# Scan stage of a fused tokenizer, state-space and expert kernel: part of the multiply by C moved from VectorE to GpSimd

## The chip, the cores and the metric

One core of one Trainium2 chip runs the whole program. The metric is the device time of one execution in microseconds (us). Of this kernel a difference of about 0.3%, or 4 us, can be told from none.

## What is computed

The reference is a model in three parts: a tokenizer over 32 images, a state-space block with a gated feed-forward, and attention with a mixture of experts. The change lies in the state-space block, in its selective scan:

```python
xdbl = jnp.einsum('bld,kd->blk', z, W_xproj)
dt_in, Bm, Cm = jnp.split(xdbl, [DT_RANK, DT_RANK + D_STATE], axis=-1)
dt = jax.nn.softplus(jnp.einsum('blr,dr->bld', dt_in, W_dt) + b_dt)
A_bar = jnp.exp(dt[..., None] * A)
Bx = (dt * z)[..., None] * Bm[:, :, None, :]
_, h = jax.lax.associative_scan(comb, (A_bar, Bx), axis=1)   # h = A_bar * h + Bx
y = jnp.einsum('blds,bls->bld', h, Cm) + D_skip * z
```

There are 16 states, an inner width of 384 and 82 tokens per sequence. Everything is float32.

## The kernel before

The 32 sequences go in 8 rounds of G = 4. A round's tokens are N = 4 x 82 = 328 columns. The inner width lies on 128 partitions in NI = 3 tiles, so that one state of a round is a row of 3 x 328 = 984 columns, cut into two halves of HALF = 492.

For each state `s` of a round the engines do this, each in a queue written out by hand:

- ScalarE (`decays`, L1208) writes exp(dt A) into PSUM, half by half, two states ahead.
- GpSimd (`inputs`, L1452) writes Bx = dtz x B into a ring of four tiles in SBUF, three states ahead.
- VectorE (`scan`, L1340) scans each half into the PSUM tile `hs`. Then (`step`, L1352) it multiplies `hs` by the row of C: first the columns 0 to 656 (semaphore `s_hm`), then 656 to 984 (`s_hc`), into one of the four tiles of `hc`. Then it scans state s+1, whose first half waits for `s_hm` and its second half for `s_hc`.
- TensorE (`add_y`, L1069) adds the two halves of `hc` into the PSUM sum of y with an identity matrix. It waits for `s_hc` once and counts `s_ys`. The ring of four keeps VectorE from writing `hc` of state s before `s_ys` has passed state s-4.

Between these steps each engine has the work of the next round (`pre`) and of the round before (`post`), placed by state number. Of it these pieces matter here. TensorE and ScalarE do theirs ahead of the step of the same state, VectorE and GpSimd behind it:

- After state 15 ScalarE copies y out of PSUM (`drain`, L1226). Only then may TensorE add state 0 of the next round (L1069). At state 1 it multiplies y by W_out (L1025), and VectorE adds the result to the input in two parts (L1316).
- At state 2 TensorE transposes (L977). At states 3, 4 and 5 it makes the gate and the input of the next round (L983, L986). ScalarE takes the tanh (L1155), and VectorE makes z of it (L1295), which frees the PSUM bank for the next one. At state 6 come the projections X (L1007), and ScalarE keeps them (L1159, L1160). At state 8 TensorE makes the step sizes D0 and D1, at state 9 D2 (L990). ScalarE takes rl and ax of each (L1133, L1134) and behind D2 also `u` (L1167).
- At states 3 and 4 ScalarE squares x1 and makes the mean (`b_ms`, L1185), and GpSimd's `post` of state 4 waits for it (`b_rr`, L1437). GpSimd's `post` of state 6 are two adds (L1441).
- GpSimd's step of state 10 waits for `u` of the next round. Behind it come the product for state 13 and then the softplus of the next round on GpSimd (L1422 to L1432), between the products for 14 and 15.
- At states 10 to 13 TensorE makes the feed-forward's gate and up parts (L983, L986), ScalarE the tanh (L1198) and VectorE the two products th and av (L1321, L1324). At state 14 TensorE makes the down projection (L1050).

Round 0 stands ahead of the loop, rounds 1 to 6 are three turns of a loop with two rounds in each, and round 7 stands behind it. SyncE loads the rows of B and C for the next round into `BC`, group by group of four states, when `s_hc` says that the old ones are read.

Of the kernel before, what the change touches and what calls it, by code (L numbers as in the profile page):

```python
# [776 lines left out]
def mamba(nc, ctx, block, at, ps, tok, fr, H, vec, ident, w_zg, w_x, w_dt, a_log, w_o, w_ug, w_dn, bc_d, xs):  # L777
# [4 lines left out]
    if True:  # L782
# [485 lines left out]
        def _(v):  # L1268
# [78 lines left out]
            def step(i, par, s, last):  # L1347
                v.wait_ge(s_scan, 2 * (i * STATE + s) + 2)
                at_least(v, s_ys, i * STATE + (s - LONG + 1))
                C = CL[:, s % GROUP, :] if par == 1 and s // GROUP == 3 else BC[:, s // GROUP, 1, s % GROUP, :]  # L1350
                for a, b, done in ((0, 2, s_hm), (2, 3, s_hc)):
                    v.tensor_tensor(hc[:, s % LONG, a:b], hs.rearrange("p (a n) -> p a n", a=NI)[:, a:b],  # L1352
                                    C.rearrange("p (a n) -> p a n", a=1).broadcast_to([128, b - a, N]), ALU.mult).then_inc(done, 1)
# [1303 lines left out]
```

## Time and profile before

| | |
|---|---|
| median of 3 runs | 1356.89 us (1353.74 to 1357.17) |
| profiled execution, its own time | 1359.36 us |
| its span | 1357.3 us |
| scan stage in it | from about 246 to 758 us |
| granted TensorE clock, mean | 0.941 |
| busy over the span | PE 88%, DVE 79%, ACT 52%, POOL 54% |

PE is TensorE, DVE is VectorE, ACT is ScalarE, POOL is GpSimd. A timeline row gives the start in us from the span's beginning, the length in us of the merged instructions, the engine, the line, the operation, its operands and the count. In brackets stands how long the engine was idle before it, and what ended that.

### The profile page before, as it was taken

Reading aid. Unit: us, or ns where it says so; the run is one execution under the profiler, and the core shown is the slowest. Engines: PE = TensorE matmul, PEld = TensorE weight load, DVE = VectorE, ACT = ScalarE, POOL = GpSimd, SP = SyncE. Lnnn points to the kernel's source line nnn. Section 1 sums busy time; section 2 is a strip of 40 time slices with the busy share of each in tenths; the row PEclk is TensorE's granted clock in tenths of the full one; section 3 lists DMA queues with packets and bytes.
Section 4 is the critical chain, followed back from the end, with each engine's and each line's share of the span. In section 5 each row is a group of like instructions: output and inputs, shape, how many; then the busy total and the mean of one; then the engine's idle time right before and its main releaser. Section 6 shows DMA issues by size and latency. Waiting matters only on the chain.

```text
span 1357.3 us, 20617 instructions
## 1 busy us (share of the span) xinstructions
PE 1192.2 (88%) x5716; PEld 754.8 (56%) x5717; DVE 1067.9 (79%) x2393; ACT 702.1 (52%) x1628; POOL 739.3 (54%) x465
## 2 busy tenths in 40 slices
PE   6985867568998889898987789999999889999996
PEld 4432434224444445455443468888888666676674
DVE  5999697989999899989999646778887646666663
ACT  1256431776776778676856345555552462233232
POOL 3047662877888686959696410135555565222322
PEclk9997878798999999999999899999997789999998
DMA  6200002651615152423430044001112133222221
GB/s 176 71 1 0 28 9 61 240 190 40 221 33 206 28 202 81 149 87 143 140 123 0 1 143 138 9 17 25 26 26 55 34 59 53 41 39 38 38 39 22
DMA packets 76919, 102.83 MB, mean 76 GB/s; under 512 B 13562, under 2 KB 65369, under 8 KB 76825
## 3 DMA queue, kind: packets, MB, share of 16 engines
q1 hardware_dynamic: 57490, 90.82, 20.4%
q0 software_dynamic: 17152, 9.24, 5.1%
q10 hardware_dynamic: 2184, 1.72, 0.5%
q8 instruction: 35, 0.57, 0.2%
q14 instruction: 58, 0.48, 0.1%
HBM read 70.23 MB, written 30.18 MB: 74 GB/s over the span
## 4 chain that ended last, share of the span: by engine, by line
PE 56%; DVE 19%; ACT 12%; issue 9%; POOL 2%; DMA 1%; DVEq 1%; SPq 0%; ACTq 0%; POOLq 0%
PE ps L1069 6%; PE ps L2298 6%; PE ps L2276 5%; DVE ps L1340 3%; PE ps L1713 3%; ACT ps L1208 3%; PE ps L1050 3%; PE ps L1655 3%; PE ps L2281 3%; PE ps L983 3%; PE ps L1728 3%; PE ps L2288 3%; PE ps L277 2%; PE ps L270 2%; DVE hc L1352 2%
## 5 line engine op out<-in xcount | busy, mean ns | idle before, releaser
L1452 POOL TENSOR_TENSOR Bx<-dtz,BC 128x984 f32<-128x984 f32 x128 | 289.6, 2288 | 77.1 <-DVE ps L1340 46.1
L1069 PE MATMUL ps<-hc,b_id 128*128 128x492 f32 x512 | 249.0, 612 | 61.6 <-DVE hc L1352 47.0
L1340 DVE TENSOR_TENSOR_SCAN ps<-ps,Bx 128x492 f32<-128x492 f32 x256 | 288.4, 1172 | 6.9 <-POOL Bx L1452 5.8
L1208 ACT ACTIVATE ps<-dt,A 128x324 f32<-128x324 f32 (+1 forms) x512 | 213.1, 457 | 51.5 <-DVE ps L1340 50.6
L1069 PEld LDWEIGHTS ps<-hc,b_id 128*128 128x128 f32 x512 | 91.8, 195 | 174.1 <-issue 120.6
L2434 POOL DMA_INDIRECT out<-yt,dest x48 | 74.8, 1558 | 160.6 <-DVE yt L2420 150.7
L2353 ACT ACTIVATE hT__6165<-ps,e_b 128x128 f32<-128x128 f32 x288 | 79.4, 374 | 154.1 <-PE ps L2288 154.0
L1352 DVE TENSOR_TENSOR hc<-ps,BC 128x656 f32<-128x656 f32 x224 | 139.1, 663 | 5.3 <-PE ps L1069 1.5
L2298 PE MATMUL ps<-W,hT__6165 128*128 x576 | 109.5, 327 | 1.1 <-DVE yb L2414 1.1
L2129 POOL DMA_INDIRECT buckets<-XS,c_slot x64 | 90.6, 1416 | 32.0 <-issue 15.8
L2298 PEld LDWEIGHTS ps<-W,hT__6165 128*128 128x128 f32 x576 | 91.7, 191 | 1.7 <-issue 1.7
L2141 POOL TENSOR_TENSOR c_x<-c_x,bro 82x192 f32<-82x192 f32 x32 | 18.9, 590 | 135.3 <-DVE c_x L1896 134.6
L2400 DVE COPY hb<-ps 128x768 f32<-128x768 f32 x41 | 39.2, 957 | 58.7 <-PE ps L2281 56.4
L2276 PE MATMUL ps<-W,xT 128*128 x192 | 78.8, 535 | 6.8 <-DVE xT L2391 2.7
L1869 DVE TENSOR_REDUCE mx<-ps 82x12 f32<-82x984 f32 x32 | 37.7, 1178 | 52.5 <-PE ps L1713 51.7
L1728 PEld LDWEIGHTS ps<-V,PT 82*82 82x82 f32 x768 | 62.5, 156 | 7.4 <-issue 1.8
L1713 PE MATMUL ps<-kB,qT 128*82 128x328 f32 (+1 forms) x256 | 61.9, 387 | 3.1 <-DVE E L1873 2.0
L1728 PE MATMUL ps<-V,PT 82*82 82x17 f32 x768 | 61.4, 226 | 0.7 <-DVE XN L1903 0.7
L579 POOL TENSOR_TENSOR DF<-DF,prod 96x392 f32<-96x392 f32 x56 | 56.6, 1010 | 4.4
L983 PE MATMUL ps<-hfT,wug 128*128 128x328 f32 x128 | 45.4, 479 | 14.5 <-DVE av L1324 13.0
L207 DVE SCALAR_TENSOR_TENSOR ps<-PF,vec,ps 96x196 f32<-96x196 f32 (+2 forms) x168 | 57.7, 424 | 0.0
L207 DVE SCALAR_TENSOR_TENSOR ps<-P,vec,ps 128x196 f32<-128x196 f32 x168 | 56.4, 421 | 0.0
(283 smaller groups left out, 2415.9 us busy)
## 6 DMA issues: line engine op xcount, KB each, us to landing
BC<-bc_rows SPq DMA_DIRECT2D x16, 1312.0 KB, 9.2
BC<-bc_rows SPq DMA_DIRECT2D x28, 656.0 KB, 6.9
buckets<-b_zero SPq DMA_DIRECT2D x8, 2288.0 KB, 14.8
xg<-buckets SPq DMA_DIRECT2D x48, 104.0 KB
xc<-in_xcol SPq DMA_DIRECT2D x4, 1176.0 KB, 9.4
W<-in_w1d SPq DMA_DIRECT2D x8, 576.0 KB, 10.2
W<-in_w2d SPq DMA_DIRECT2D x8, 576.0 KB, 10.3
CL<-bc_rows SPq DMA_DIRECT2D x4, 656.0 KB, 8.2
```

The costliest lines, as they stand in the source:

```text
L207: i = eng.scalar_tensor_tensor(flat(dst[:, k, cols]) if t == 8 else acc, tap(src, k, c, t, a, b), w, acc, ALU.mult, ALU.add)
L983: pe.matmul(ps[:, banks[k], 0:N], w[:, k, c_], x[:, 0, :], start=True, stop=False)
L1069: mm = pe.matmul(ps[:, BANK_Y + h, 0:HALF], ident[:], f2(hc[:, s % LONG])[:, h * HALF:(h + 1) * HALF], start=s == 0, stop=s == STATE - 1)
L1208: a = act.activation(ps[:, BANK_A + h, c:c + w].rearrange("p (g t) -> p g t", t=S)[:, :, 1:S], dt[:, (par + t // STATE) % 2, m, g0 * S:g1 ...
L1340: v.tensor_tensor_scan(hs[:, c], ps[:, BANK_A + h, 0:HALF], f2(Bx[:, t % RING])[:, c], 0.0, ALU.mult, ALU.add).then_inc(s_scan, 1)
L1352: v.tensor_tensor(hc[:, s % LONG, a:b], hs.rearrange("p (a n) -> p a n", a=NI)[:, a:b], C.rearrange("p (a n) -> p a n", a=1).broadcast_to( ...
L1452: g.tensor_tensor(Bx[:, t % RING], dtz[:, p], BC[:, t % STATE // GROUP, 0, t % GROUP, :].rearrange("p (a n) -> p a n", a=1).broadcast_to([ ...
L1713: mm = pe.matmul(ps[0:S, SCORES + h0 // 6, (h0 % 6) * S:(h0 % 6 + h1 - h0) * S], qT[:, par, m_, q * S:(q + 1) * S], kB[:, par, m_, q, j:j ...
L1728: mm = pe.matmul(ps[0:S, HEAD_OUT + c % 2, h * (DH + 1):(h + 1) * (DH + 1)], PT[:, c % 2, h, :], V[:, vpar, c, h, :], start=True, stop=True)
L2129: g.indirect_dma_start(out=xs, out_offset=bass.IndirectOffsetOnAxis(ap=slot[:, p % 2, k, c:c + 1], axis=0), in_=slots(p)[:, c, :], in_offs ...
L2276: pe.matmul(ps[:, UP + h, 0:384], xT[:, p, 0, :], W1[:, bass.ds(e, 1), h * 384:(h + 1) * 384].rearrange("p a n -> p (a n)"), start=True, s ...
L2298: mm = pe.matmul(ps[:, Y, 0:D], hT[:, p, k, :], W2[:, k, bass.ds(e, 1), :].rearrange("p a n -> p (a n)"), start=k == 0, stop=k == KF - 1)
```

## The change

In the seven states of `POOLED` the second half is scanned straight into the tile of `hc` in SBUF. VectorE multiplies only the first half, in two instructions of 328 and 164 columns. GpSimd multiplies the second half in place, in two instructions of 164 and 328 columns. It does so at its step of the next state, ahead of the product Bx that stood there, and counts `s_hp`. TensorE waits for `s_hp` between the two halves of such a state. The first half scan behind a state of `POOLED` waits for `s_hc` instead of `s_hm`, and the second half scan of a state of `POOLED` has to wait for its tile of `hc` (`s_ys`) itself. SyncE waits for `s_hp` too before it loads new rows of C.

```diff
+        POOLED = (0, 1, 2, 3, 5, 7, 8)
...
+        def pooled(i, s):
+            return i * len(POOLED) + sum(k < s for k in POOLED)
...
                 for h in range(2):
+                    if h == 1 and s in POOLED:
+                        pe.wait_ge(s_hp, pooled(i, s) + 1)
                     mm = pe.matmul(ps[:, BANK_Y + h, 0:HALF], ident[:], f2(hc[:, s % LONG])[:, h * HALF:(h + 1) * HALF],
...
-                    at_least(v, s_hc if h else s_hm, i * STATE + t)
+                    at_least(v, s_hc if h or (t - 1) % STATE in POOLED else s_hm, i * STATE + t)
+                    direct = h == 1 and t % STATE in POOLED
+                    if direct:
+                        at_least(v, s_ys, i * STATE + (t - LONG + 1))
                     c = slice(h * HALF, (h + 1) * HALF)
-                    v.tensor_tensor_scan(hs[:, c], ps[:, BANK_A + h, 0:HALF], f2(Bx[:, t % RING])[:, c],
+                    v.tensor_tensor_scan((f2(hc[:, t % LONG]) if direct else hs)[:, c], ps[:, BANK_A + h, 0:HALF], f2(Bx[:, t % RING])[:, c],
                                          0.0, ALU.mult, ALU.add).then_inc(s_scan, 1)
...
+                if s in POOLED:
+                    v.tensor_tensor(out[:, 0:N], hs[:, 0:N], C, ALU.mult).then_inc(s_hm, 1)
+                    v.tensor_tensor(out[:, N:HALF], hs[:, N:HALF], C[:, 0:HALF - N], ALU.mult).then_inc(s_hc, 1)
...
             def step(i, par, s, last):
+                if s - 1 in POOLED:
+                    C, out = rows_c(par, s - 1), f2(hc[:, (s - 1) % LONG])
+                    g.wait_ge(s_scan, 2 * (i * STATE + s))
+                    g.tensor_tensor(out[:, HALF:2 * N], out[:, HALF:2 * N], C[:, HALF - N:N], ALU.mult)
+                    g.tensor_tensor(out[:, 2 * N:3 * N], out[:, 2 * N:3 * N], C, ALU.mult).then_inc(s_hp, 1)
```

The two places of which the prediction speaks most are GpSimd's queue from the start of a round to its wait for b_ms and beyond, and TensorE's queue at states 7 to 9. First GpSimd, in a turn of the loop, before: the products for states 4, 5 and 6, then b_rr.

```order
79 L1452 TENSOR_TENSOR Bx<-dtz,BC 128x984 [waits b_scan]
80 L1447 ISA
81 L640 ISA [waits b_BC1]
82 L1452 TENSOR_TENSOR Bx<-dtz,BC 128x984 [waits b_scan]
83 L640 ISA
84 L1452 TENSOR_TENSOR Bx<-dtz,BC 128x984 [waits b_scan]
85 L640 ISA
86 L1452 TENSOR_TENSOR Bx<-dtz,BC 128x984 [waits b_scan]
87 L640 ISA
88 L1452 TENSOR_TENSOR Bx<-dtz,BC 128x984 [waits b_scan]
89 L1437 TENSOR_TENSOR b_rr<-b_ms,b_nh 82x4 [waits b_mss]
```

And now, from behind the pair for state 0 on: before each product stands a pair of multiplies by C.

```order
101 L1471 TENSOR_TENSOR Bx<-dtz,BC 128x984 [waits b_scan,b_BC1]
102 L1485 ISA
103 L1486 TENSOR_TENSOR hc<-hc,BC 128x164 [waits b_scan]
104 L1487 TENSOR_TENSOR hc<-hc,BC 128x328
105 L1471 TENSOR_TENSOR Bx<-dtz,BC 128x984 [waits b_scan]
106 L1485 ISA
107 L1486 TENSOR_TENSOR hc<-hc,BC 128x164 [waits b_scan]
108 L1487 TENSOR_TENSOR hc<-hc,BC 128x328
109 L1471 TENSOR_TENSOR Bx<-dtz,BC 128x984 [waits b_scan]
```

Four pairs now stand ahead of b_rr, for the states 0 to 3. The pairs for 5, 7 and 8 stand between b_rr and the wait for u.

TensorE at states 7 to 9, before: add_y of state 7, D0 and D1, add_y of state 8, D2.

```order
195 L1065 REGISTER_ALU
196 L1069 MATMUL ps<-hc,b_id 128x492 x2
197 L990 MATMUL ps<-dtin,wdt 128x328 x2
198 L1065 REGISTER_ALU
199 L1069 MATMUL ps<-hc,b_id 128x492 x2
200 L990 MATMUL ps<-dtin,wdt 128x328
```

And now:

```order
219 L1075 REGISTER_ALU
220 L1081 MATMUL ps<-hc,b_id 128x492
221 L1080 REGISTER_ALU
222 L1081 MATMUL ps<-hc,b_id 128x492
223 L1000 MATMUL ps<-dtin,wdt 128x328 x2
224 L1075 REGISTER_ALU
225 L1081 MATMUL ps<-hc,b_id 128x492
226 L1080 REGISTER_ALU
227 L1081 MATMUL ps<-hc,b_id 128x492
228 L1000 MATMUL ps<-dtin,wdt 128x328
```

The two halves of a state are now parted by a register operation and the wait for GpSimd, and D0, D1 and D2 stand behind such waits.

## Rows read from the trace of the kernel before

**Rows 1.** The page's chain that ended last, shares by engine.

```profile
PE 56%; DVE 19%; ACT 12%; issue 9%; POOL 2%; DMA 1%; DVEq 1%; SPq 0%; ACTq 0%; POOLq 0%
```

**Rows 2.** Windows, u to u: length, busy PE, PEld, DVE, ACT, POOL, clock, DMA.

```profile
479.75:542.39 62.64, 58.23 (x213) 31.41 (x212) 60.54 (x80) 47.46 (x112) 51.56 (x24) 1.00 0.36 124
542.39:609.66 67.27, 59.74 (x213) 32.03 (x212) 60.84 (x80) 47.20 (x112) 51.54 (x25) 0.97 0.34 116
```

**Rows 3.** Groups by shape, VectorE in the scan stage; count, then busy us, mean ns.

```profile
L1352 DVE TENSOR_TENSOR hc<-ps,BC 128x656 f32<-128x656 f32 x112 | 93.6, 836 | 5.3 <-PE ps L1069 1.5 <-issue 1.2
L1352 DVE TENSOR_TENSOR hc<-ps,BC 128x328 f32<-128x328 f32 x112 | 54.8, 489 | 0.0
```

**Rows 4.** Timeline of GpSimd, from the start of round 4 to u.

```profile
497.03 18.04 POOL L1452 TENSOR_TENSOR Bx<-dtz,BC 128x984 f32<-128x984 f32 x8
517.99 2.28 POOL L1452 TENSOR_TENSOR Bx<-dtz,BC 128x984 f32<-128x984 f32 x1 [2.92 <-DVE ps L1340]
523.29 1.02 POOL L1437 TENSOR_TENSOR b_rr<-b_ms,b_nh 82x4 f32<-82x4 f32 x1 [3.02 <-ACT b_ms L1185]
528.80 1.97 POOL L1441 TENSOR_TENSOR x<-x,H 82x384 f32<-82x384 f32 x2
530.72 4.50 POOL L1452 TENSOR_TENSOR Bx<-dtz,BC 128x984 f32<-128x984 f32 x2
542.39 2.32 POOL L1452 TENSOR_TENSOR Bx<-dtz,BC 128x984 f32<-128x984 f32 x1 [4.10 <-ACT u L1167]
```

**Rows 5.** Line 1441's view: GpSimd's queue, duration ns min/median/max.

```profile
L1441 POOLq FUSED_REGOPS  x12: 60/60/60, 334.7 to 657.4; - x12
```

**Rows 6.** Timeline of VectorE, the same round.

```profile
505.77 1.23 DVE L1352 TENSOR_TENSOR hc<-ps,BC 128x656 f32<-128x656 f32 x2
506.92 2.25 DVE L1340 TENSOR_TENSOR_SCAN ps<-ps,Bx 128x492 f32<-128x492 f32 x2
514.03 0.55 DVE L1316 TENSOR_TENSOR x<-xl,ps 82x384 f32<-82x384 f32 x1 [0.88 <-PE ps L1025]
533.69 2.25 DVE L1340 TENSOR_TENSOR_SCAN ps<-ps,Bx 128x492 f32<-128x492 f32 x2
535.98 1.25 DVE L1352 TENSOR_TENSOR hc<-ps,BC 128x656 f32<-128x656 f32 x2
```

**Rows 7.** Timeline of TensorE, the same round.

```profile
508.21 1.89 PE L1069 MATMUL ps<-hc,b_id 128*128 128x492 f32 x4 [1.17 <-ACT y L1226]
509.93 4.06 PE L1025 MATMUL ps<-wo,y 128*82 128x192 f32 x24
521.81 1.37 PE L983 MATMUL ps<-hT,wzg 128*128 128x328 f32 x4
539.03 0.72 PE L990 MATMUL ps<-dtin,wdt 96*128 96x328 f32 x2
```

**Rows 8.** Timeline of ScalarE, the same round.

```profile
521.40 0.85 ACT L1208 ACTIVATE ps<-dt,A 128x162 f32<-128x162 f32 x2 [0.21 <-DVE ps L1340]
531.33 0.44 ACT L1159 ACTIVATE BCs<-ps 32x328 f32<-32x328 f32 x1 [1.66 <-PE ps L1007]
540.22 0.53 ACT L1133 ACTIVATE rl<-ps,vec 128x328 f32<-128x328 f32 x1
541.20 1.02 ACT L1167 ACTIVATE u<-ax 128x984 f32<-128x984 f32 x1
```

**Rows 9.** Timelines of GpSimd and TensorE at rounds 0, 5 and 7.

```profile
245.83 17.90 POOL L1452 TENSOR_TENSOR Bx<-dtz,BC 128x984 f32<-128x984 f32 x8 [2.29 <-DVE dtz L1309]
...
285.18 2.32 POOL L1452 TENSOR_TENSOR Bx<-dtz,BC 128x984 f32<-128x984 f32 x1 [3.93 <-ACT u L1167]
...
590.56 1.02 POOL L1437 TENSOR_TENSOR b_rr<-b_ms,b_nh 82x4 f32<-82x4 f32 x1 [3.03 <-ACT b_ms L1185]
...
609.66 2.28 POOL L1452 TENSOR_TENSOR Bx<-dtz,BC 128x984 f32<-128x984 f32 x1 [4.10 <-ACT u L1167]
...
734.24 1.27 PE L983 MATMUL ps<-hfT,wug 128*128 128x328 f32 x4
```

More of the change, by code:

```diff
@@ L822, in mamba @@
         s_w1 = sem("b_w1"); s_c1 = sem("b_c1"); s_sp = sem("b_sp"); s_dt = sem("b_dt"); s_dtz = sem("b_dtz")
-        s_ab = sem("b_ab"); s_bx = sem("b_bx"); s_scan = sem("b_scan"); s_hc = sem("b_hc"); s_hm = sem("b_hm"); s_ys = sem("b_ys"); s_skip = sem("b_skip"); s_y = sem("b_y")
+        s_ab = sem("b_ab"); s_bx = sem("b_bx"); s_scan = sem("b_scan"); s_hc = sem("b_hc"); s_hm = sem("b_hm"); s_hp = sem("b_hp"); s_ys = sem("b_ys"); s_skip = sem("b_skip"); s_y = sem("b_y")
         s_o = sem("b_o"); s_x1 = sem("b_x1"); s_sq = sem("b_sqs"); s_ms = sem("b_mss"); s_rr = sem("b_rr2"); s_hf = sem("b_hf"); s_tr2 = sem("b_tr2")
@@ L832, in f2, with rows_c @@
             return t.rearrange("p a b -> p (a b)")
+        def pooled(i, s):
+            return i * len(POOLED) + sum(k < s for k in POOLED)
+        def rows_c(par, s):
+            return CL[:, s % GROUP, :] if par == 1 and s // GROUP == 3 else BC[:, s // GROUP, 1, s % GROUP, :]
         SIDE_TILES = [("O0", 0, s_x1, 2, 1), ("O1", 0, s_x1, 2, 2), ("RT0", 1, s_hT, 2, 1), ("RT1", 1, s_hT, 2, 2),
@@ L922, in _ @@
                     sp.wait_ge(s_hc, old + 4)
+                    sp.wait_ge(s_hp, pooled(j - 1, 4))
                 spread(0)
@@ L929, in _ @@
                     sp.wait_ge(s_hc, old + 8)
+                    sp.wait_ge(s_hp, pooled(j - 1, 8))
                 spread(1)
@@ L938, in _ @@
                     sp.wait_ge(s_hc, old + 12)
+                    sp.wait_ge(s_hp, pooled(j - 1, 12))
                 spread(2, slice(1, 2))
@@ L1349, in step @@
                 at_least(v, s_ys, i * STATE + (s - LONG + 1))
[L1350 to L1353, printed above, removed]
+                C, out = rows_c(par, s), f2(hc[:, s % LONG])
+                if s in POOLED:
+                    v.tensor_tensor(out[:, 0:N], hs[:, 0:N], C, ALU.mult).then_inc(s_hm, 1)
+                    v.tensor_tensor(out[:, N:HALF], hs[:, N:HALF], C[:, 0:HALF - N], ALU.mult).then_inc(s_hc, 1)
+                else:
+                    for a, b, done in ((0, 2, s_hm), (2, 3, s_hc)):
+                        v.tensor_tensor(hc[:, s % LONG, a:b], hs.rearrange("p (a n) -> p a n", a=NI)[:, a:b],
+                                        C.rearrange("p (a n) -> p a n", a=1).broadcast_to([128, b - a, N]), ALU.mult).then_inc(done, 1)
                 if not last or s + 1 < STATE:
```

## Prediction

> **What bounds the scan stage now.** I read the chain that ended last first. It is a chain of TensorE more than of VectorE [rows 1], although the windows show VectorE busy for 60.5 of 62.6 us of a round and TensorE for 58.2 [rows 2]. So I looked for what ties one round to the next, in the timelines of one round, number 4. The tie is `u`: GpSimd stands idle for 4.10 us until ScalarE has it [rows 4], then makes the softplus and, 17.3 us later, the product for state 15, for which VectorE's scan of state 15 waits. From there two paths lead to the next `u`. One is VectorE's scans and multiplies. The other is TensorE's: y out of PSUM at 508.21, state 0, the W_out product at 509.93, the gates, X, and then ScalarE from 531.33 to u at 541.20 [rows 7, 8]. That stretch of ScalarE shows no idle time in front of its rows behind the first, so only an earlier X or an earlier D2 could move u, and X hangs on TensorE's queue. VectorE waits 0.88 us for the W_out product at 514.03 [rows 6]. A lighter VectorE alone would therefore wait more there and gain little. GpSimd has waits of 2.92, 3.02 and 4.10 us in the round [rows 4], which is the room that the change wants to use. A round takes 62.6 us, or 67.3 where the loop turns [rows 2].
>
> **What VectorE saves.** The multiply of 656 columns takes 836 ns and that of 328 takes 489 ns, so a column costs 1.06 ns [rows 3]. 492 columns less are 0.52 us per state. The first scan now waits for the second multiply: without a wait it starts 0.08 us before the listed end (505.77 + 1.23 against 506.92), with one an instruction starts 0.04 us behind it (533.69 + 2.25 against 535.98) [rows 6]. That takes 0.12 us back. Net 0.4 us per state, 2.8 per round, 22 over the eight rounds, all of it beside the path above except in round 7. A scan into SBUF instead of PSUM is in no row for this shape; I price it at no difference, with bounds of 0.1 us either way, for which VectorE's room is the cover.
>
> By the Trainium skill, page "VectorE: DVE Perf Modes", section "The DRAIN you can't avoid", a semaphore wait on the engine's own last operation costs nothing extra. The rows here show 0.12 us; by the page VectorE would save 29 us instead of 22, and the forecast would stay, since that time is not on the path.
>
> **What GpSimd gets.** Products of 984 columns follow each other at 18.04 / 8 = 2.255 us, adds of 384 at 1.97 / 2 = 0.985 us [rows 4]. A straight line through both gives 0.17 us plus 2.12 ns per column: 0.52 and 0.87 us, a pair 1.39. The listed sums contain the tail of the last instruction, so I take 1.35. Bounds: 1.13 us, which is half a product of 984 columns with no fixed cost at all, and 1.97 us, two instructions at the price of the 384-column adds. Seven pairs are 9.5 us in each round on an engine that was busy for 51.6 of 62.6: 61.0 of 62.6.
>
> The page "GPSIMD Engine Reference" of the Trainium skill, sections 3.1 and 4.1, says that two-input elementwise work takes GpSimd 2.6 cycles per element and should stay on VectorE. At the 4497 ns it gives for 2048 columns, an estimate for a pair without fixed cost is 1.08 us. The rows give 1.35; by the page the sum below would be some 3 us smaller.
>
> **Where the pairs stand on the path, round 4.**
> 1. State 0. GpSimd makes five products from 497.03 to 508.3, then the pair, to 509.65. TensorE wants the second half in the middle of 508.21 to 509.93, at 509.05 [rows 7]. It starts 0.65 us late, with a handover of 0.05. The W_out product and VectorE's x1 at 514.03 follow, +0.65. Up to X, 0.25 of it is won back: the gate at 521.81 waited for z on VectorE, which now comes earlier. So X and BCs at 531.33 are 0.4 late, and u could not be less than 0.4 late.
> 2. b_rr. Products and four pairs take GpSimd from 497.03 to 522.7, so it still waits for b_ms. That stands behind the decays at 521.40, which waited for the scan [rows 8]. ScalarE starts its piece 0.65 late but no longer waits, so b_rr comes at about 523.7 instead of 523.29.
> 3. States 5, 7, 8. From b_rr to the end of the two products at 530.72 + 4.50 it was 11.9 us. With three pairs it is 16.0, so the pair of state 8 ends at 539.7. The pairs of states 1, 2, 3 and 5 are done before TensorE wants them; state 7's is about 2 us late but D0 and D1 still arrive when ScalarE gets to them.
> 4. D2. TensorE takes the second half at 539.75, 0.85 us, and D2 starts at 540.6 instead of 539.03 [rows 7] and ends at 541.15. ScalarE's rl, at 540.22 before [rows 8], starts at 541.15. **u, and with it the round, is 0.9 us later.** VectorE's 2.8 us become waits: for the decays, for th and av, and for Bx of state 15.
>
> **The other rounds.** Where the loop turns (1, 3, 5), y is copied later than GpSimd is done with state 0, so step 1 costs nothing, and b_rr comes 0.2 earlier, at 590.35, by the 0.21 that the decays waited for the scan [rows 8, 9]. Then 16.0 + 0.9 + 0.6 put the end of D2 at 607.85; rl stood at 609.66 - 2.17 = 607.49, by the distance of rows 4 and 8. That is +0.35 each. Round 0 has no b_rr: 245.83 + 12 x 2.255 + 7 x 1.35 = 282.3, D2 ends at 283.75, and u reaches GpSimd 2.1 us later, at 285.9 instead of 285.18 [rows 9], +0.7. In round 7 the first feed-forward gate at 734.24 stands behind the same queue and comes 1.7 us later; VectorE had 1.2 us of room before it needed that gate, so +0.45.
>
> **Sum.** 0.7 + 3 x 0.35 + 3 x 0.9 + 0.45 = 4.9 us. To it come TensorE's new register operations between the halves: a register operation on a queue takes 60 ns [rows 5], five per round lie on TensorE's path, so between 0 and 8 x 0.3 = 2.4 us; I take 1. Together **+6 us**. SyncE's new waits cost nothing: the rows of C that they guard are for the next round, more than 20 us off. The profiled execution took 1359.4 (span 1357.3) and would take 1365; the median of the runs is 2.5 us below that execution, so I predict **1363 us**, 0.4% slower. A measurement of this kernel can tell about 0.3% from no change, 4 us; "same" below means within that. A pair of 1.13 us instead of 1.35 takes some 0.65 off at D2: only the floor of 0.4 in rounds 2, 4, 6 and nearly nothing else are left, 1358. A pair of 1.97 makes GpSimd arrive at b_rr behind b_ms: 2 x 0.6 for the pairs and 1.8 behind it, about +3.5 per round, 1385.
>
> **Rivals.**
> - *Faster: the pair of state 8 is no obstacle.* If a pair took under about 0.85 us, state 0's would end by 509.1 and state 8's before 538.2, where TensorE wants it (D2's 539.03 less 0.85), and no wait would be left on the path. Then the earlier z and the earlier scan win some 0.3 us in each of seven rounds, and round 7, where little but VectorE counts, gains its 2.8. That is 5 us, 1352. For it: GpSimd's idle time of 10 us a round is as long as the seven pairs. Against it: 1.13 us is the least that the rows allow. If I am wrong about TensorE and ScalarE holding u, part of VectorE's 22 us would show too, down to 1335. Chance 0.18.
> - *No change: the waits cancel.* Pairs near 1.13 us, or b_ms earlier than I think, so that the delays fall below 0.4 us a round. 1358. Chance 0.30.
> - *Much slower: the pairs are dear.* GpSimd and VectorE hold each other up in SBUF, or each short instruction costs 0.3 us more. From a pair of 1.5 us on GpSimd is late at b_rr too and bounds every round. At 2 us a pair it is 1388. Against it: the products ran at 2.25 us each while VectorE was busy 97% of the time. Chance 0.10. [...]
> - *The change doesn't do what it says.* The queues show the pairs and the waits, so I give this nothing.
>
> **How the numbers follow.** The forecast itself, slower by 4 to 20 us, has 0.42. Faster by over 0.3%: 0.18. Within: 0.30. Slower: 0.42 + 0.10 = 0.52. The range of the forecast alone is 1361 to 1377. For 8 in 10 I go from 1350, below the first rival's 1352 but not to its 1335, to 1379, short of the dear pairs.
>
> **What would show it.** Right: GpSimd's idle before u falls from 4.1 us to about 1; waits of TensorE's L1081 and its weight loads for GpSimd's hc at states 7 and 8; D2 about 1.5 us later after b_rr; VectorE with some 3 us of new idle time a round; rounds of 63.5 and 67.6 us; pairs of 0.5 and 0.85 us. Wrong: a round shorter than 62.6 us; no wait for hc of GpSimd on TensorE; GpSimd's wait before b_rr gone, which would mean that the pairs are dearer.

## The result, and the profile after

The changed kernel takes **1367.22 us** (median of 5 runs, 1364.68 to 1369.88) against 1356.89 (5 runs, 1352.55 to 1360.88). The ratio is 1.0083, 95% interval 1.0061 to 1.0106: 0.8% slower, +10.3 us, where +6 was forecast. The profiled execution took 1369.88 us, span 1368.0; it is the slowest of the five runs. (One execution of the experiment e1 took 1449 us at a mean granted clock of 0.809, against 0.93 to 0.95 in all others, and is left out of its ratio.)

The chain that ended last, after. GpSimd's share has gone from 2% to 20% [rows 1].

```profile
PE 46%; POOL 20%; DVE 14%; issue 11%; ACT 6%; DMA 1%; DVEq 0%; POOLq 0%; SPq 0%; ACTq 0%
```

Windows after, u to u, with the columns of [rows 2]: a round is 1.1 us longer, or 0.4 where the loop turns. VectorE has lost 2.65 us of work (60.54 to 57.89) and GpSimd has gained 9.1.

```profile
481.52:545.25 63.73, 57.97 (x213) 31.36 (x212) 57.89 (x80) 47.12 (x112) 60.67 (x39) 1.00 0.37 122
545.25:612.89 67.64, 59.11 (x213) 32.05 (x212) 57.90 (x80) 47.02 (x112) 60.64 (x38) 0.97 0.34 116
```

Groups by shape after, in the scan stage. The two GpSimd multiplies have 0.54 and 0.88 us; in the timeline they start 0.50 apart and the next instruction 0.84 later, so a pair occupies 1.34 (1.35 was taken). The scan into SBUF is not slower than the one into PSUM: the 56 are all second halves and most of the 199 first ones, but the distance from the start of a state's first scan to its multiply is 2.28 us with it and 2.29 without.

```profile
L1355 DVE TENSOR_TENSOR_SCAN ps<-ps,Bx 128x492 f32<-128x492 f32 x199 | 227.8, 1178 | 20.8 <-ACT ps L1220 12.6 <-POOL Bx L1471 3.3 <-DVE hc L1368 0.9
L1355 DVE TENSOR_TENSOR_SCAN hc<-ps,Bx 128x492 f32<-128x492 f32 x56 | 64.6, 1154 | 0.0
L1487 POOL TENSOR_TENSOR hc<-hc,BC 128x328 f32<-128x328 f32 x56 | 49.4, 881 | 0.0
L1486 POOL TENSOR_TENSOR hc<-hc,BC 128x164 f32<-128x164 f32 x56 | 29.9, 535 | 10.2 <-DVE hc L1355 10.2
```

Waits after, rounds 1 to 6: engine, line, what it waited for, us in total, times, longest. These two rows have no counterpart before.

```profile
PEld ps L1081 <- POOL hc L1487: 26.5, 21, 2.4
PE ps L1081 <- POOL hc L1487: 13.2, 15, 1.6
```

VectorE after, the multiplies of one state and the scan behind them. From the first multiply to the scan it is 0.83 us, before it was 1.15 [rows 6].

```profile
507.59 0.49 DVE L1367 TENSOR_TENSOR hc<-ps,BC 128x328 f32<-128x328 f32 x1
508.00 0.32 DVE L1368 TENSOR_TENSOR hc<-ps,BC 128x164 f32<-128x164 f32 x1
508.42 1.19 DVE L1355 TENSOR_TENSOR_SCAN ps<-ps,Bx 128x492 f32<-128x492 f32 x1
```

Timeline of GpSimd after, round 4, which answers to [rows 4]: the pair of state 0, b_rr, the pair of state 8, Bx behind u, and the softplus's first row.

```profile
509.96 0.55 POOL L1486 TENSOR_TENSOR hc<-hc,BC 128x164 f32<-128x164 f32 x1
510.46 0.90 POOL L1487 TENSOR_TENSOR hc<-hc,BC 128x328 f32<-128x328 f32 x1
...
525.41 1.03 POOL L1456 TENSOR_TENSOR b_rr<-b_ms,b_nh 82x4 f32<-82x4 f32 x1 [1.09 <-ACT b_ms L1197]
...
539.97 0.52 POOL L1486 TENSOR_TENSOR hc<-hc,BC 128x164 f32<-128x164 f32 x1
540.47 0.87 POOL L1487 TENSOR_TENSOR hc<-hc,BC 128x328 f32<-128x328 f32 x1
...
545.25 2.30 POOL L1471 TENSOR_TENSOR Bx<-dtz,BC 128x984 f32<-128x984 f32 x1 [1.69 <-ACT u L1179]
547.51 3.52 POOL L1441 TENSOR_SCALAR ax<-u 128x984 f32<-128x984 f32 x1
```

Timeline of TensorE after, the same round, which answers to [rows 7]: state 0, the W_out product, states 7 and 8, D2. The waits of 0.19, 1.59 and 0.53 us are for GpSimd's multiplies. The pair of state 8 ends at 541.34, TensorE goes on at 541.38, and D2 stands right behind it.

```profile
510.16 1.06 PE L1081 MATMUL ps<-hc,b_id 128*128 128x492 f32 x2 [1.17 <-ACT y L1238]
511.41 1.09 PE L1081 MATMUL ps<-hc,b_id 128*128 128x492 f32 x2 [0.19 <-POOL hc L1487]
512.34 4.06 PE L1035 MATMUL ps<-wo,y 128*82 128x192 f32 x24
...
537.83 1.09 PE L1081 MATMUL ps<-hc,b_id 128*128 128x492 f32 x2 [1.59 <-POOL hc L1487]
...
541.38 1.09 PE L1081 MATMUL ps<-hc,b_id 128*128 128x492 f32 x2 [0.53 <-POOL hc L1487]
542.31 0.72 PE L1000 MATMUL ps<-dtin,wdt 96*128 96x328 f32 x2
```

**Where the 10 us come from.** I take the distance between the softplus's first rows on GpSimd (`ax<-u`, the last row of the fence above) as the length of a round, count round 0 from its first Bx, and end round 7 at the memset of kB. In us:

| round | 0 | 1 | 2 | 3 | 4 | 5 | 6 | 7 | stage |
|---|---|---|---|---|---|---|---|---|---|
| before | 41.8 | 64.3 | 62.7 | 67.4 | 62.7 | 67.2 | 62.7 | 81.8 | 510.5 |
| after | 43.8 | 65.3 | 63.7 | 69.1 | 63.7 | 67.6 | 63.7 | 84.4 | 521.3 |
| difference | 2.0 | 1.0 | 1.05 | 1.7 | 1.05 | 0.4 | 1.0 | 2.6 | 10.8 |
| forecast | 0.7 | 0.35 | 0.9 | 0.35 | 0.9 | 0.35 | 0.9 | 0.45 | 4.9 + 1 |

All of the loss is in the scan stage: what stands before and behind it took 846.7 us in both profiled executions (245.8 + 600.9 and 241.9 + 604.8). That rest is the same program in every kernel here, yet it varied from 838.8 (e1) to 850.9 us (e6) between profiled executions. So the stage is compared by its own length, and the kernels by the ratios of many runs.

Rounds 2, 4, 5 and 6 went nearly as forecast. The excess is in rounds 0, 1, 3 and 7. In 1, 3 and 7 rows of TensorE stand at a lower clock than before; in round 0 it is a wait. The end of round 7, TensorE after:

```profile
729.01 1.09 PE L1081 MATMUL ps<-hc,b_id 128*128 128x492 f32 x2 [0.44 <-DVE hc L1368]
732.42 2.74 PE L1081 MATMUL ps<-hc,b_id 128*128 128x492 f32 x4 [2.31 <-POOL hc L1487]
735.97 2.01 PE L1081 MATMUL ps<-hc,b_id 128*128 128x492 f32 x2 [0.81 <-POOL hc L1487]
737.77 3.03 PE L1074 MATMUL ps<-z,skip 128*128 128x328 f32 x8
...
742.28 1.27 PE L993 MATMUL ps<-hfT,wug 128*128 128x328 f32 x4
```

The skip product took 1.82 us before and takes 3.03 here; two additions of 492 columns take 2.01 instead of 1.09. The granted clock of this stretch, after (first window) and before (second, in a fence of its own), is 0.81 against 1.00, which is a mixture of the levels 2.4 and 1.2 GHz:

```profile
727.00:745.00 18.00, 14.43 (x41) 7.21 (x40) 14.20 (x19) 8.92 (x21) 17.88 (x13) 0.81 0.00 0
```

```profile
722.00:741.00 19.00, 15.45 (x52) 7.45 (x52) 18.83 (x24) 10.48 (x24) 15.34 (x10) 1.00 0.00 1
```

The feed-forward gate, at 742.28, is 63.45 us behind its round's softplus row; before it was 734.24 - 674.58 = 59.66 [rows 9]. VectorE then waits for th:

```profile
744.81 0.50 DVE L1333 SCALAR_TENSOR_TENSOR th<-th,ps 128x328 f32<-128x328 f32 x1 [3.40 <-ACT th L1210]
```

In round 0 TensorE reaches the pair of state 0 before GpSimd has it. The rows of TensorE after:

```profile
252.21 4.64 PE L1081 MATMUL ps<-hc,b_id 128*128 128x492 f32 x6 [2.79 <-POOL hc L1487]
256.69 0.73 PE L987 MATMUL ps<-b_id,hn 82*128 82x82 f32 x8
```

The transposition is now 256.69 - 241.90 = 14.8 us behind the round's first Bx, where it was 257.43 - 245.83 = 11.6. ScalarE's copy of it stands ahead of decays that VectorE needs, so VectorE waits 2.96 us at 259.72.

### The profile page after: what moved, and what is told of

Same layout as the page of the kernel before. It is cut to its first block, busy times and chain, and to the rows that moved or that the text cites. A ratio compares the mean times of both kernels' runs of the same rounds, so it can differ in the third digit from the quotient of the medians.

```text
span 1368.0 us, 20809 instructions
## 1 busy us (share of the span) xinstructions
PE 1198.4 (88%) x5716; PEld 759.3 (56%) x5717; DVE 1045.3 (76%) x2393; ACT 699.9 (51%) x1628; POOL 812.0 (59%) x577
## 3 DMA queue, kind: packets, MB, share of 16 engines
q10 hardware_dynamic: 2184, 1.72, 0.5%
## 4 chain that ended last, share of the span: by engine, by line
PE 46%; POOL 20%; DVE 14%; issue 11%; ACT 6%; DMA 1%; DVEq 0%; POOLq 0%; SPq 0%; ACTq 0%
POOL Bx L1471 11%; PE ps L2322 6%; PE ps L2300 5%; PE ps L1679 3%; PE ps L1737 3%; PE ps L2305 3%; PE ps L1752 3%; PE ps L2312 3%; PE ps L277 2%; PE ps L1081 2%; POOL hc L1487 2%; PE ps L270 2%; DVE ps L207 2%; ACT prod L398 2%; POOL hc L1486 2%
## 5 line engine op out<-in xcount | busy, mean ns | idle before, releaser
L1081 PE MATMUL ps<-hc,b_id 128*128 128x492 f32 x512 | 256.4, 620 | 70.3 <-POOL hc L1487 22.4
L1355 DVE TENSOR_TENSOR_SCAN ps<-ps,Bx 128x492 f32<-128x492 f32 x200 | 229.0, 1178 | 23.3 <-ACT ps L1220 12.6
L1220 ACT ACTIVATE ps<-dt,A 128x324 f32<-128x324 f32 (+1 forms) x512 | 210.5, 456 | 43.5 <-DVE ps L1355 40.1
L1371 DVE TENSOR_TENSOR hc<-ps,BC 128x656 f32<-128x656 f32 x112 | 69.5, 661 | 0.8
L1355 DVE TENSOR_TENSOR_SCAN hc<-ps,Bx 128x492 f32<-128x492 f32 x56 | 64.6, 1154 | 0.0
L1752 PE MATMUL ps<-V,PT 82*82 82x17 f32 x768 | 62.3, 227 | 0.7 <-DVE XN L1927 0.7
```

Source lines behind the costliest of these rows:

```text
L1220: a = act.activation(ps[:, BANK_A + h, c:c + w].rearrange("p (g t) -> p g t", t=S)[:, :, 1:S], dt[:, (par + t // STATE) % 2, m, g0 * S:g1 ...
L1355: v.tensor_tensor_scan((f2(hc[:, t % LONG]) if direct else hs)[:, c], ps[:, BANK_A + h, 0:HALF], f2(Bx[:, t % RING])[:, c], 0.0, ALU.mult, ...
L1752: mm = pe.matmul(ps[0:S, HEAD_OUT + c % 2, h * (DH + 1):(h + 1) * (DH + 1)], PT[:, c % 2, h, :], V[:, vpar, c, h, :], start=True, stop=True)
```

## The experiments

Times are medians; ratios are to the kernel before, run beside it on the same chip. Its own median was 1354.88 for e1 to e4, 1355.53 for e5 to e8, 1355.34 for e9 to e11 and 1357.67 for e12. To place a cost I divide round 4 into three pieces, at the W_out product and at b_rr; they are the first three columns. All numbers are distances between rows of GpSimd's and TensorE's timelines, in us:

| kernel | softplus to W_out | W_out to b_rr | b_rr to next softplus | stage | ratio |
|---|---|---|---|---|---|
| before | 27.93 | 13.36 | 21.38 | 510.5 | 1 |
| after | 28.54 | 13.07 | 22.10 | 521.3 | 1.0083 |
| e1 light VectorE | 27.18 | 13.05 | 21.22 | 501.8 | 0.9936 |
| e2 no TensorE wait | 27.37 | 13.16 | 21.12 | 502.6 | 0.9943 |
| e3 half later | 26.91 | 13.55 | 21.41 | 507.8 | 0.9991 |
| e4 without 7, 8 | 28.54 | 13.07 | 21.23 | 519.4 | 1.0045 |
| e5 only 5, 7, 8 | 28.08 | 13.36 | 22.04 | 514.9 | 1.0075 |
| e6 half later, 2 3 5 7 8 | 27.61 | 13.06 | 21.91 | 511.3 | 1.0006 |
| e7 pair of 8 twice | 29.15 | 13.07 | 23.47 | 535.7 | 1.0215 |
| e8 half later, 2 3 4 5 7 8 | 29.27 | 13.07 | 21.70 | 516.9 | 1.0084 |
| e9 half later, 0 1 2 3 5 | 26.77 | 13.67 | 21.33 | 505.9 | 0.9942 |
| e10 without 0 | 28.09 | 13.07 | 22.05 | 515.0 | 1.0044 |
| e11 half later, without 7 | 26.70 | 13.76 | 21.26 | 508.4 | 0.9992 |
| e12 half later, 0 to 3 | 26.65 | 13.85 | 21.26 | 506.4 | 0.9952 |

### e1: VectorE's saving alone

```diff
-                    if h == 1 and s in POOLED:
-                        pe.wait_ge(s_hp, pooled(i, s) + 1)
...
-                if s - 1 in POOLED:
...
-                    g.tensor_tensor(out[:, HALF:2 * N], out[:, HALF:2 * N], C[:, HALF - N:N], ALU.mult)
-                    g.tensor_tensor(out[:, 2 * N:3 * N], out[:, 2 * N:3 * N], C, ALU.mult).then_inc(s_hp, 1)
```

> The second half of the seven states is not multiplied by C at all: GpSimd's pairs, TensorE's waits for them and SyncE's are left out, VectorE's work stays as in the changed kernel. Theory (TensorE and ScalarE set the round, VectorE does not): little is won although VectorE has 22 us less work. Rounds from u to u of 62.3 to 62.6 us instead of 62.6, round 7 shorter by 2 to 3 us, together 4 to 7 us faster than before, about 1351. Rival A (VectorE sets the round): some 20 us faster, 1337. Rival B (the cost lies in VectorE's own new order, the scan that waits for the second multiply and the scans into SBUF): as slow as the changed kernel, 1367.

Measured: 1344.73 us, ratio 0.9936 (0.9914 to 0.9958), 9 to 10 us faster than before, more than the 4 to 7 expected. The stage is 8.7 us shorter, and each of rounds 2, 4 and 6 takes 61.45 instead of 62.68, where 62.3 to 62.6 were expected. So the saving is worth more than the 5 us that the first rival gave it, and far less than VectorE saves, which is 0.33 us a state or 18 us.

### e2: all the work, but TensorE doesn't wait for it

```diff
-                    if h == 1 and s in POOLED:
-                        pe.wait_ge(s_hp, pooled(i, s) + 1)
-                    mm = pe.matmul(ps[:, BANK_Y + h, 0:HALF], ident[:], f2(hc[:, s % LONG])[:, h * HALF:(h + 1) * HALF],
+                    mm = pe.matmul(ps[:, BANK_Y + h, 0:HALF], ident[:], f2(hc[:, s % LONG])[:, 0:HALF],
...
+                        at_least(v, s_hp, pooled(i + t // STATE, max(0, t % STATE - 3)))
```

> GpSimd makes all pairs in place as in the changed kernel, but TensorE adds the first half twice in place of the second, so it reads nothing of GpSimd's and has no wait for it; VectorE waits for the pair of four states ago instead, which is long done. Theory (the waits in TensorE's queue cost the time, not GpSimd's load): about as fast as the kernel with no pairs, 1351 to 1355, GpSimd's wait for u down to some 0.3 us. Rival (GpSimd's load of 61 us a round sets it, or holds VectorE up in SBUF): as slow as the changed kernel, 1364 to 1367, and scans or multiplies of VectorE longer than with no pairs.

Measured: 1346.73 us, ratio 0.9943 (0.9923 to 0.9962), within 2 us of e1 and faster than the 1351 to 1355 expected. GpSimd makes all its pairs and is nearly full; its wait for u falls to 0.69 us:

```profile
535.12 2.33 POOL L1471 TENSOR_TENSOR Bx<-dtz,BC 128x984 f32<-128x984 f32 x1 [0.69 <-ACT u L1177]
```

GpSimd's load by itself costs next to nothing. The 1.4% between this kernel and the changed one, some 19 us, are what the waits in TensorE's queue bring with them.

### e3: the second half added one step later

```diff
+                if s - 1 in POOLED:
+                    pe.wait_ge(s_hp, pooled(i, s - 1) + 1)
+                    half(s - 1, 1)
...
-                for h in range(2):
-                    if h == 1 and s in POOLED:
-                        pe.wait_ge(s_hp, pooled(i, s) + 1)
...
-                mm.then_inc(s_ys, 1)
+                half(s, 0)
+                if s not in POOLED:
+                    half(s, 1)
```

> The whole computation. TensorE takes the second half of a pooled state one step later, ahead of the first half of the next state, so D2 and the transposition stand ahead of the wait for the pair instead of behind it. Theory: D2 is no longer held up, u comes as before or 0.1 to 0.3 us earlier, rounds of 62.4 to 62.7 and 67.0 to 67.3 us, and round 7 gains 1 to 2 us: 1352 to 1356, that is 11 to 15 us below the changed kernel. Rival (any wait for GpSimd in TensorE's queue costs the same, wherever it stands, because GpSimd is behind): 1364 to 1367.

Measured: 1352.33 us, ratio 0.9991 (0.9973 to 1.0009). The whole computation stays, with the same seven pairs, and the loss is gone. The third column (b_rr to softplus) is back at 21.41. The only wait for a pair in round 4 behind the W_out product now stands behind D2 (at 533.73), where it can't hold u:

```profile
534.91 1.09 PE L1070 MATMUL ps<-hc,b_id 128*128 128x492 f32 x2 [0.37 <-POOL hc L1493]
```

### e4: without the pairs of states 7 and 8

```diff
-        POOLED = (0, 1, 2, 3, 5, 7, 8)
+        POOLED = (0, 1, 2, 3, 5)
```

> POOLED = (0, 1, 2, 3, 5), the whole computation. Theory (the pairs of 7 and 8 hold up D2, state 0's costs 0.4 us in rounds 2, 4 and 6 and about 2 us in round 0 through the transposition at state 2): rounds of 63.0 and 67.3 us, round 7 shorter than before by about 1, together +1 to +4 us, 1358 to 1361. Rival (cost in proportion to GpSimd's load): 5 of 7 pairs, +7 us, 1364.

Measured: 1359.80 us, ratio 1.0045 (1.0029 to 1.0062). The first two columns of the table are those of the changed kernel to a hundredth, and the third falls from 22.10 to 21.23: steps 3 and 4 of the prediction stand for 0.87 us a round. The trace also has the clock at work. Rounds 2 and 4 have the same wait for the pair of state 0 and the same addition ahead of the W_out product. In round 2 the clock falls, in round 4 not:

```profile
378.75 1.77 PE L1081 MATMUL ps<-hc,b_id 128*128 128x492 f32 x2 [0.64 <-POOL hc L1487]
380.31 5.11 PE L1035 MATMUL ps<-wo,y 128*82 128x192 f32 x24
```

```profile
511.37 1.09 PE L1081 MATMUL ps<-hc,b_id 128*128 128x492 f32 x2 [0.64 <-POOL hc L1487]
512.29 4.06 PE L1035 MATMUL ps<-wo,y 128*82 128x192 f32 x24
```

That is 1.05 us on the product and 0.68 on the addition, and round 2 lasts 64.5 us where round 4 lasts 62.8. Round 6 is like round 2: 4.93 us for the product, 64.6 for the round.

### e5: only the pairs of 5, 7 and 8

```diff
-        POOLED = (0, 1, 2, 3, 5, 7, 8)
+        POOLED = (5, 7, 8)
```

> POOLED = (5, 7, 8), the whole computation; the complement of the run without 7 and 8. Theory (the pairs of 7 and 8 stand ahead of D2): round 0 about 0.5 us shorter than before, since GpSimd is not behind there, rounds 2, 4 and 6 at 63.2, rounds 1, 3 and 5 0.3 us longer, round 7 1 to 2.5 us longer with TensorE's clock down behind its waits: +3 to +5 us, 1358 to 1360. Rival (only the load of GpSimd counts, 3 of 7 pairs, or only state 0's wait does): no slower than before.

Measured: 1364.73 us, ratio 1.0075 (1.0050 to 1.0100). That is above the 1358 to 1360 expected, though rounds 2, 4 and 6 have 63.5 us (63.2 expected) and round 7 is only 0.7 longer than before (1 to 2.5 expected). It is the counterpart of e4: the first half of the round is near the kernel before (41.44 against 41.29), the third column has the full 22.04. Its stage is 6.4 us shorter than the changed kernel's, but the ratio is nearly as bad. The profiled executions stand at opposite ends here: e5's is the fastest of its four runs, the changed kernel's the slowest of its five.

### e6: second half later, without states 0 and 1

```diff
-        POOLED = (0, 1, 2, 3, 5, 7, 8)
+        POOLED = (2, 3, 5, 7, 8)
```

(on top of e3)

> TensorE takes second halves one step later as in the run before, and POOLED = (2, 3, 5, 7, 8), the whole computation. Theory: VectorE's savings in states 0 and 1 are lost anyway, since it waits there for the W_out product, while their pairs make GpSimd late in round 0. Round 0 1 to 2 us shorter than with seven pairs, the rounds 2, 4 and 6 at 61.6 to 61.9, round 7 no longer: 3 to 6 us below the kernel before, 1349 to 1352. Rival (each pooled state gives its share, two of seven given up): 1354, between the run with seven and the kernel before.

Measured: 1356.29 us, ratio 1.0006 (0.9982 to 1.0029). A miss: 1349 to 1352 was expected, since I had taken the pairs of states 0 and 1 for a burden. They are one in rounds 0 and 1, which are 2.6 us shorter here than in e3 together, and a gain in rounds 2, 4 and 6, which are 0.7 us longer each. In the table the piece to the W_out product grows from 26.91 to 27.61, because the second half of state 0 is again ahead of the product, and the third from 21.41 to 21.91. The stage is 3.5 us longer than in e3, but 2.4 of it are in round 7, where the skip product ran at the lower clock (2.91 us against 1.82 in e3). By the intervals of the ratios e6 and e3 can't be told apart.

### e7: the pair of state 8 made twice

```diff
+                    if s - 1 == 8:
+                        g.tensor_tensor(out[:, HALF:2 * N], out[:, HALF:2 * N], C[:, HALF - N:N], ALU.mult)
+                        g.tensor_tensor(out[:, 2 * N:3 * N], out[:, 2 * N:3 * N], C, ALU.mult).then_inc(s_hq, 1)
+                        g.wait_ge(s_hq, i + 1)
```

> The changed kernel, but GpSimd multiplies the second half of state 8 twice by C (so y has C squared there), one pair of 1.4 us more in each round. Theory (the end of this pair sets D2, u and the round): each of the eight rounds 1.4 us longer than in the changed kernel, rounds 2, 4, 6 at 65.1, +11 us over it, 1378. Rival (GpSimd still has 1.7 us of idle time before u, which takes it up; the cost lies in the early pairs): within 2 us of the changed kernel, 1366 to 1368.

Measured: 1384.85 us, ratio 1.0215 (1.0193 to 1.0237), 17.6 us above the changed kernel where 11 was expected. The second pair moves GpSimd by 1.46 us (548.83 to 550.29), TensorE's wait for state 8 grows from 0.53 to 1.97, and the third column by 1.37:

```profile
546.71 1.09 PE L1081 MATMUL ps<-hc,b_id 128*128 128x492 f32 x2 [1.55 <-POOL hc L1491]
...
551.71 1.09 PE L1081 MATMUL ps<-hc,b_id 128*128 128x492 f32 x2 [1.97 <-POOL hc L1491]
```

So this pair lies on the path with its whole length. The other 0.61 us of the round stand ahead of the W_out product, and they come through the feed-forward's first gate, which stands behind D2 and the skip product. That product ran at the lower clock at the end of round 3 (2.92 us, 1.82 in the changed kernel):

```profile
487.45 2.92 PE L1074 MATMUL ps<-z,skip 128*128 128x328 f32 x8
```

The gate then starts 0.25 us before the softplus row instead of 1.31, VectorE gets th 2.27 us behind that row instead of 1.22, and the first addition of round 4 comes 1.06 us later (27.42 against 26.36). 0.45 of it is won back, since TensorE no longer waits for the pair of state 0. Rounds 2 and 6 show the same; round 7, ahead of which the skip product took 1.82 us, has its first addition at 26.34.

### e8: second half later, with a pair for state 4

```diff
-        POOLED = (2, 3, 5, 7, 8)
+        POOLED = (2, 3, 4, 5, 7, 8)
```

(on top of e6)

> As the run with later second halves and (2, 3, 5, 7, 8), with state 4 pooled too. Theory: the pair of 4 stands behind b_rr and makes the pairs of 7 and 8 1.4 us later, which holds up the first half of state 8 and D2 by some 0.5 us, as much as VectorE's 0.4 us gives: 0 to 3 us above that run. Rival (VectorE sets the round once the waits are gone): 2 to 3 us below it.

Measured: 1364.24 us, ratio 1.0084 (1.0061 to 1.0107): 8 us above e6, where 0 to 3 was expected. The third column is even a little shorter than in e6. GpSimd works through it without a single wait, so its own load is the limit there, although TensorE waits 0.69 us for the pair of state 7 ahead of D2. The 1.66 us are in the first column, so they belong to what stands behind u. TensorE in e8, then in e6:

```profile
536.19 0.72 PE L1000 MATMUL ps<-dtin,wdt 96*128 96x328 f32 x2
537.99 1.09 PE L1070 MATMUL ps<-hc,b_id 128*128 128x492 f32 x2 [1.08 <-POOL hc L1493]
...
542.22 1.27 PE L993 MATMUL ps<-hfT,wug 128*128 128x328 f32 x4
```

```profile
535.95 1.09 PE L1070 MATMUL ps<-hc,b_id 128*128 128x492 f32 x2
...
540.19 1.27 PE L993 MATMUL ps<-hfT,wug 128*128 128x328 f32 x4
```

TensorE waits 1.08 us for the pair of state 8 behind D2, and the feed-forward's first gate stands behind it. The gate starts 0.18 us before the softplus row (542.40), in e6 1.72 before (541.91). VectorE then waits 1.64 us for th, and all that remains of the round is 1.5 us later. A late pair costs at whichever of two places it reaches, D2 or the next gate; in e7 it is both.

### e9, e11, e12: the second half later, and which pairs

All three are the kernel of e3 with another list: e9 (0, 1, 2, 3, 5), e11 (0, 1, 2, 3, 5, 8), e12 (0, 1, 2, 3).

> The kernel of e3 (second half added one step later) with the pairs of states 7 and 8 left to VectorE as before the change: pairs of states 0, 1, 2, 3 and 5, whole computation. In e3 ScalarE's u still held GpSimd 1.0 us in round 4, and TensorE still waited 0.4 us for a pair at 534.9 us; both lie in the piece from b_rr to u, where the pairs of 7 and 8 stand. If what is left of the cost is those two pairs: rounds 2, 4, 6 fall from 61.9 to about 61.5, as in e1, and the time to 3 to 6 us under the kernel before, ratio 0.996 to 0.998. If VectorE's saving in states 7 and 8 is worth as much as the pairs cost: no difference from e3, ratio 0.998 to 1.000.

> The kernel of e3 with the pair of state 7 alone left to VectorE: pairs of 0, 1, 2, 3, 5 and 8, whole computation. GpSimd has 1.35 us less between b_rr and u than in e3, so that its wait for u should grow from 1.0 to about 2.4 us and nothing else change if GpSimd is not what u waits for. If GpSimd's order between b_rr and u is what sets u (the pair of state 8 ends b_rr + 16 in the changed kernel): the pair of 8 comes 1.35 earlier and rounds 2, 4, 6 fall to about 61.5; time 2 to 5 us under the kernel before. If not, within 2 us of e3's ratio: 0.998 to 1.000.

> The kernel of e9 without the pair of state 5: pairs of states 0 to 3, second half added one step later, whole computation. In e9 the four states before b_rr have TensorE's order unblocked and b_rr waits for nothing; the pair of state 5 stands between b_rr and u. If pairs after b_rr cost by themselves (as those of 7 and 8 did, 11 us from e3 to e9 in the profiled executions' neighbourhood, some 0.15 us per round in the trace), this is 0 to 3 us faster than e9: ratio to before 0.992 to 0.995, rounds 2, 4, 6 at 61.5 to 61.7. If VectorE's saving of 0.4 us in state 5 is on the path: 61.9 to 62.1 per round, ratio 0.995 to 0.998.

Measured: e9 1347.46 us, ratio 0.9942 (0.9922 to 0.9962); e11 1354.07, 0.9992 (0.9974 to 1.0010); e12 1350.31, 0.9952 (0.9931 to 0.9973). **e9 does the whole computation and is faster than both kernels**, 0.6% under the one before and 1.4% under the changed one; e12's interval overlaps e9's, so state 5's pair is worth nothing that can be told. In e9 no wait for a pair is left on TensorE in round 4, and GpSimd's wait for u is long again:

```profile
506.35 1.06 PE L1070 MATMUL ps<-hc,b_id 128*128 128x492 f32 x2 [1.17 <-ACT y L1244]
507.25 4.06 PE L1035 MATMUL ps<-wo,y 128*82 128x192 f32 x24
```

```profile
520.92 1.06 POOL L1462 TENSOR_TENSOR b_rr<-b_ms,b_nh 82x4 f32<-82x4 f32 x1
...
539.97 2.32 POOL L1477 TENSOR_TENSOR Bx<-dtz,BC 128x984 f32<-128x984 f32 x1 [3.54 <-ACT u L1185]
```

The time of e9 is better than the 3 to 6 us under the kernel before that I expected, but not for the reason given: 61.5 us per round was not met, it has 61.77, e3 61.87. In the traces e9's stage is 1.9 us shorter than e3's, nearly all in round 7 (79.8 against 81.5); in the runs the gap is 5 to 7 us. In e11 GpSimd's wait for u grew from 1.04 to 2.25 us, as it should if u doesn't wait for GpSimd, and the time stayed that of e3; so the third column is not set by the pairs once TensorE adds them later. Of the 2.5 us by which e11's stage is longer than e9's, 2.1 are in round 7, where e11's skip product ran at the lower clock (2.62 us). Why its runs are 6.6 us above e9's is open. In the profiled executions 4.6 us lie outside the stage (842.3 us in e9 with 1348.2 of span, 846.9 in e11 with 1355.3).

### e10: the changed kernel without the pair of state 0

```diff
-        POOLED = (0, 1, 2, 3, 5, 7, 8)
+        POOLED = (1, 2, 3, 5, 7, 8)
```

> The changed kernel without the pair of state 0 (1, 2, 3, 5, 7, 8 stay), whole computation, TensorE's order as in the change. It tests step 1 of the prediction (TensorE reaches the output projection 0.65 us later because of state 0's pair, of which 0.4 reach b_rr) and the term that was missing in round 0. By step 1: rounds 2, 4, 6 0.3 to 0.5 us shorter than the change's 63.7, minus 0.4 of VectorE's saving that goes too, so 63.6 to 63.8, and round 0 shortens by 1 to 1.5 us (wait of 2.8 us for the pair of state 0 gone): time 2 to 4 us under the change, ratio to before 1.005 to 1.007. If state 0 costs nothing by itself: 1366 to 1369 us, ratio 1.007 to 1.010.

Measured: 1361.20 us, ratio 1.0044 (1.0026 to 1.0062), 5 to 6 us under the change. The W_out product comes 0.45 us earlier, nothing else in the round moves, and rounds 2, 4 and 6 take 63.2 us, 0.5 less than in the changed kernel. I had expected 63.6 to 63.8 per round since VectorE's saving in state 0 goes too. It goes at no cost: in this order it is not on the path. Round 0 is 1.3 us shorter, 42.5 us.

## Why the prediction was right and where it was wrong

**Right: direction, mechanism and the normal round.** The path from y over W_out, X and D2 to u set the rounds, as forecast. Step by step, in round 4:

- The pair took 1.34 us, forecast 1.35. The estimate of 1.08 from the Trainium skill's page "GPSIMD Engine Reference", section 3.1, has no fixed cost in it; the trace has the two multiplies start 0.50 us apart at 164 columns, and decides. (That such a pair would make the sum "some 3 us smaller" doesn't fit the prediction's own 1358 for a pair of 1.13, which is 5 less.)
- Step 1: W_out 0.65 late was forecast; it is 28.54 - 27.93 = 0.61. 0.25 won back up to X; 13.36 - 13.07 = 0.29. e10 takes the pair of state 0 away and gets 0.45 back.
- Step 2: b_rr 0.4 late; +0.32. It still waits for b_ms, 1.09 us.
- Step 3: the pair of state 8 was to end 16.0 us behind b_rr; 541.34 - 525.41 = 15.9. The pair of state 7 held TensorE for 1.59 us, and here ScalarE waited 0.61 us for D0, where the step said that D0 and D1 would arrive in time.
- Step 4: D2 16.9 us behind b_rr was forecast (540.6 - 523.7); 542.31 - 525.41 = 16.9. ScalarE's rl started 0.76 us behind D2 and not 0.55. The round is 1.05 us longer, forecast 0.9. e4 and e5 show this step alone: 0.87 and 0.66 us.
- VectorE's saving was 0.33 us a state and not 0.4, 18 us and not 22: the scan that waits for the second multiply starts 0.10 us behind its listed end (508.42 against 508.00 + 0.32), where 0.04 was taken. It changes nothing in the sum, which had this saving off the path.
- A scan into SBUF costs nothing extra (2.28 us from scan to multiply against 2.29). The rival of dear pairs has fallen with it and with the pair's 1.34. By the Trainium skill, page "SBUF — State Buffer", section "Who interferes with whom", a VectorE instruction with at most one SBUF input and outside the two-port modes doesn't hold up GpSimd; the trace agrees, with a pair no dearer than forecast.
- The named signs hold: GpSimd's wait before u fell from 4.10 to 1.69 us, TensorE waits for hc at states 7 and 8, VectorE's idle time per round grew from 2.1 to 5.8 us (some 3 more were forecast), rounds of 63.7 and (round 5) 67.6 us were forecast as 63.5 and 67.6.

**Wrong: three terms of the sum.** Between the 4.9 us of the rounds in the forecast and the 10.8 of the traces these terms make 5.4.

- *Round 0, "+0.7"*: it is +2.0. The term counted GpSimd's instructions up to D2 and left out that step 1 applies there and more so: TensorE waits 2.79 us for the pair of state 0, the transposition comes 3.2 us later, and VectorE waits 2.96 us behind it. e5, e6 and e8, which have no pairs for states 0 and 1, have rounds 0 of 41.0, 41.0 and 40.1 us against 43.8, and e10, which lacks only the pair of state 0, has 42.5, the forecast +0.7.
- *Round 7, "+0.45"*: it is +2.6. The queue was right, the size not. The gate was to come 1.7 us later and comes 3.8 later. The additions and the skip product behind the waits ran largely at the lower clock: 0.8 and 0.9 us on the six additions, 1.2 on the skip product.
- *Rounds 1 and 3, "+0.35 each, y is copied later than GpSimd is done with state 0"*: +1.0 and +1.7. In round 1 that sentence fails, TensorE waits 0.77 us for the pair; in both the W_out product ran slower, 5.18 us instead of 4.48 and 5.42 instead of 4.08. In round 5, where it took 4.07 us and there was no wait, the term was met (+0.4).

I priced a wait of TensorE by its length, and the sum took every matmul from rows at the full clock. In round 7 the two can be told apart. e10 has the same pairs and a wait as long there, but the clock did not fall, and its round 7 is 81.9 us; e5's is 82.5, also with the full clock behind a wait of 2.32 us. The forecast was 82.25. TensorE in e10:

```profile
729.85 1.92 PE L1081 MATMUL ps<-hc,b_id 128*128 128x492 f32 x4 [2.30 <-POOL hc L1487]
733.40 1.09 PE L1081 MATMUL ps<-hc,b_id 128*128 128x492 f32 x2 [1.63 <-POOL hc L1487]
734.33 1.82 PE L1074 MATMUL ps<-z,skip 128*128 128x328 f32 x8
```

So the queue and the waits of round 7 were priced rightly, and the fall of the clock made the other 2 us. What makes it fall is open. In round 7 the skip product was slow in four kernels (this one, e6, e7 and e11), each behind a wait of 2.15 to 2.5 us for a pair, and never where the waits were shorter; but e5 and e10 have such a wait and the full clock. e4's rounds 2 and 4 have the same wait, and one fell while the other did not. And a wait for GpSimd is not needed: e1 and e2 have none on TensorE, and where the loop turns (rounds 3 and 5) their W_out products took 4.69 and 5.10, 4.79 and 4.94 us. In round 3 of the changed kernel no such wait stands ahead of the slow product either. So what the slow products add to rounds 1 and 3 can't be put down to the pairs.

The term of 1 us for TensorE's register operations is not seen: the distances of steps 1 and 4 came out without it.

**The first rival's size was wrong too.** It gave 5 us if no wait remained. e1 and e2 give 8 to 10. Per round e1 gains 1.06 us up to b_rr, 0.75 of it ahead of the W_out product (y is ready earlier) and 0.31 behind it (z earlier). I had allowed 0.3, the second part alone, and thought a lighter VectorE would only wait more at W_out. Its condition (a pair under 0.85 us) was worked out for this order of TensorE's queue and was not tested; with TensorE taking the result one step later, a pair of 1.34 is no obstacle. In e9 the 0.85 us gained up to b_rr come in three parts: 0.34 by an earlier y (the first addition 25.87 us behind the softplus row, before 26.21), 0.3 by an earlier z (e6 has 13.06 there, with both halves ahead of W_out), and the rest by the second half of state 0 being added behind the W_out product instead of ahead of it. That last part needs no GpSimd at all; the kernel before with this alone was not tried.
